# A graph layer on one core: who takes the mixed tiles out of PSUM and adds them to the rows

## What is computed

```python
xn = _layernorm(x, axis=-1)
x = x + _L0_gnn_ref(xn, edge_index, edge_weight, node_vec1) + _L0_mix_ref(xn[None], ...)[0]
x = x + _L0_ffn_ref(_layernorm(x, axis=-1)[None], ...)[0]
```

## Time and profile before

| what | us |
|---|---|
| median of 3 runs | 2407.29 (2406.35 to 2408.89) |
| the profiled execution: its time | 2410.31 |
| the profiled execution: its span | 2408.5 |
| front and setup, up to the first sort's hot_t | 0 to 247 |
| first sorts (with the mixed tiles from 267) | 247 to 382 |
| main loop and last units | 382 to 1905 |
| routing | 1905 to 1984 |
| experts | 1984 to 2408.5 |

### The profile page before, as it was taken

The page is one execution under the profiler, slowest core; times in us unless marked ns, Lnnn a source line. Parts: engine busy times, 40 slices in busy tenths (PEclk is TensorE's granted clock), DMA queues, the critical chain, the costliest instruction groups (busy, mean ns, idle before and its releaser), DMA issues. The chain is left out here.

```text
span 2408.5 us, 48312 instructions
## 1 busy us (share of the span) xinstructions
PE 2151.9 (89%) x16542; PEld 1889.3 (78%) x16543; DVE 2055.8 (85%) x3323; ACT 1214.5 (50%) x1686; POOL 1613.3 (67%) x1364
## 2 busy tenths in 40 slices
PE   3887579999999999999999999999999719999893
PEld 2555467888888888888888888888889619989893
DVE  5776889999999999999999999999888596666662
ACT  1222665555555555555555555555223146666661
POOL 1665005777777777777777777777777437888883
PEclk8998789999999999999999999999999869999997
DMA  6332333333322333333233333323355454444455
GB/s 168 83 84 61 97 105 108 90 91 95 93 89 89 93 90 89 91 98 91 89 94 88 89 90 99 92 89 87 106 153 148 138 147 81 76 77 77 75 76 135
DMA packets 167330, 235.54 MB, mean 98 GB/s; under 512 B 61084, under 2 KB 128007, under 8 KB 166948
## 3 DMA queue, kind: packets, MB, share of 16 engines
q0 software_dynamic: 70896, 164.43, 27.1%
q1 hardware_dynamic: 89584, 68.67, 9.7%
q10 hardware_dynamic: 6724, 0.83, 0.4%
HBM read 186.72 MB, written 53.51 MB: 100 GB/s over the span
## 5 line engine op out<-in xcount | busy, mean ns | idle before, releaser
L775 POOL DMA_INDIRECT picked<-xn_dram,place x1029 | 1160.7, 1128 | 506.5 <-issue 298.0
L851 PE MATMUL bank<-picked,pick_w 128*128 128x256 f32 x2058 | 500.4, 379 | 4.4 <-DMA picked<-xn_dram,place 4.4
L963 ACT COPY stage<-bank 128x512 f32<-128x512 f32 x343 | 200.5, 585 | 509.9 <-PE bank L839 495.4
L851 PEld LDWEIGHTS bank<-picked,pick_w 128*128 128x128 f32 x2058 | 390.9, 190 | 58.2 <-DVE pick_w L1154 5.1
L917 ACT COPY field_rep<-fields 128x1666 bf16 (+2 forms) x235 | 397.6, 1714 | 0.1
L847 PE MATMUL bank<-window,stage 128*128 128x256 f32 x1568 | 384.2, 388 | 0.0
L1147 DVE TENSOR_TENSOR hot_w<-hots,cur 128x1536 bf16<-128x1536 bf16 x343 | 328.6, 958 | 11.9
L847 PEld LDWEIGHTS bank<-window,stage 128*128 128x128 f32 x1568 | 284.8, 192 | 31.1
L1143 DVE TENSOR_TENSOR hots<-iota_j,cur 128x1408 bf16<-128x1408 bf16 x343 | 303.3, 884 | 0.0
L839 PE MATMUL bank<-hot_w,hots 128*128 128x128 bf16 x4116 | 287.2, 220 | 11.4 <-DVE hot_w L1147 7.6
L839 PEld LDWEIGHTS bank<-hot_w,hots 128*128 128x128 bf16 x4116 | 255.3, 99 | 47.4 <-DVE hot_w L1147 8.7
(11 more groups left out here) (245 smaller groups left out, 3396.6 us busy)
## 6 DMA issues: line engine op xcount, KB each, us to landing
picked<-xn_dram,place POOLq DMA_INDIRECT x1029
xn_dram<-xn SPq DMA_DIRECT2D x49, 128.0 KB, 1.7
xT_dram<-xT SPq DMA_DIRECT2D x49, 128.0 KB, 1.8
base_dram<-acc SPq DMA_DIRECT2D x7, 896.0 KB, 7.8
sum_dram<-acc SPq DMA_DIRECT2D x7, 896.0 KB, 4.4
z_dram<-vals SPq DMA_DIRECT2D x7, 896.0 KB, 8.5
out_dram<-sum_dram SPq DMA_DIRECT2D x1, 6250.0 KB, 22.0
w_all<-in_L_ffn_W_dram SPq DMA_DIRECT2D x8, 512.0 KB, 10.1
```

Of the source, the lines that this page charges most:

```text
L775: pool.indirect_dma_start(out=picked[:, i % SETS * PICK + q, :], out_offset=None, in_=xn_dram, in_offset=bass.IndirectOffsetOnAxis(ap=plac ...
L851: mm = pe.matmul(sum_ps[pp], pick_w[i % SETS][:, q, :], picked[:, i % SETS * PICK + q, :], start=False, stop=(q == PICK - 1))
L963: act.copy(block_sb[pp].rearrange("p j c -> p (j c)"), banks[pp][:, :]).then_inc(a_copied, 1)
```

## The change

Three things are changed in `edge_sum`. DVE's `add_mix` is removed at all its places. ACT gets `take_mix(t)`, which copies the bank to one of four buffers `mix_sb` in SBUF; these lie in hot_w2 and hot_w3, which the main loop first writes behind its wait for the stores. ACT's `sort` calls it three times ahead of the ranks, twice ahead of the tiles and twice ahead of the next fields. POOL adds the buffer to the row in acc, for all 49 tiles, ahead of the first gather, which now stands behind 49 adds rather than 42. PE waits for ACT's copy (`mix_taken`) where it waited for the add; ACT's copy of tile t waits for POOL's add of tile t - 4.

```diff
+        mix_sb = [hot_w[2 + i // 2][:, :, :, :].rearrange("p f j c -> p (f j c)").bitcast(F32)[:, i % 2 * D:(i % 2 + 1) * D] for i in range(4)]
...
         @block.gpsimd
         def _(pool):
-            pool.wait_ge(mix_added, (GRP - 1) * BU)
+            for t in range(NT):
+                pool.wait_ge(mix_taken, t + 1)
+                pool.tensor_tensor(acc[:, t, :], acc[:, t, :], mix_sb[t % 4], ALU.add).then_inc(mix_added, 1)
+            pool.wait_ge(mix_added, NT)
             for t in range(NG * NT):
...
                 if t >= 4:
-                    pe.wait_ge(mix_added, t - 3)
+                    pe.wait_ge(mix_taken, t - 3)
...
             def begin():
                 make_table(AHEAD - 1)
-                pe.wait_ge(mix_added, NT)
+                pe.wait_ge(mix_taken, NT)
                 blocks(0, 0, 0)
...
+            def take_mix(t):
+                act.wait_ge(mixed, t + 1)
+                if t >= 4:
+                    act.wait_ge(mix_added, t - 3)
+                act.copy(mix_sb[t % 4], mix_ps[t % 4]).then_inc(mix_taken, 1)
+
             def sort(s):
+                t = (s - 1) * BU
                 take_base(s)
...
+                for i in range(3 if s > 0 else 0):
+                    take_mix(t + i)
                 repeat_ranks(s)
+                for i in range(3, 5 if s > 0 else 3):
+                    take_mix(t + i)
                 repeat_tiles(s + 1)
+                for i in range(5, BU if s > 0 else 5):
+                    take_mix(t + i)
                 repeat_fields(s + 1, 0, 2)
...
-            def add_mix(t):
-                dve.wait_ge(mixed, t + 1)
-                dve.tensor_tensor(acc[:, t, :], acc[:, t, :], mix_ps[t % 4], ALU.add).then_inc(mix_added, 1)
-
             def sort(s):
-
-
-                t = (s - 1) * BU
                 in_row(s)
-                if s > 1:
-                    add_mix(t - 2)
-                    add_mix(t - 1)
                 rank_ahead(s)
                 rank(s)
                 values(s, 0, 2)
-                if later(s):
-                    add_mix(t)
-                    add_mix(t + 1)
                 values(s, 2, 4)
-                if later(s):
-                    add_mix(t + 2)
-                    add_mix(t + 3)
                 values(s, 4, FIELDS)
                 slots(s)
-                if later(s):
-                    add_mix(t + 4)
                 hot_tiles(s + 1)
...
             def begin():
-                add_mix(NT - 2)
-                add_mix(NT - 1)
                 dve.wait_ge(cur_done, 2)
```

More of the change, by code:

```diff
@@ L665, in turn_ps @@
             return banks[2 if n > LATE and n % 2 == 0 else 7][:, 0:D]
-        xT_in = [sem(f"xT_in{i}") for i in range(2)]; mixed = sem("mixed"); mix_added = sem("mix_added")
+        xT_in = [sem(f"xT_in{i}") for i in range(2)]; mixed = sem("mixed"); mix_taken = sem("mix_taken"); mix_added = sem("mix_added")
         small_in = sem("small_in"); z_out = [sem(f"z_out{i}") for i in range(2)]; stat_done = sem("stat_done")
```

## The result

The change makes the kernel slower: median 2418.39 us (2413.49 to 2421.28, 6 runs) against 2409.18 us for the kernel before in the same comparisons (2406.35 to 2411.80, 6 runs). The ratio is 1.0038, 95% interval 1.0025 to 1.0051, so +9.2 us. The profiled execution has a span of 2419.5 us, 11.0 more than the one before.

What follows compares the result with a forecast made beforehand. The sorts were taken as bound by a closed PE and DVE loop of 17.1 us. Six loops +7.0, last sort +1.0, late gathers +1.0 sum to +9.0: 2407.3 + 9.0 = 2416.3 us; own range 2409 to 2425, with rivals 2396 to 2424.

Steps and rivals of the forecast that it cites:

- The three terms of the sum: Six sort loops +7.0 us, the last sort +1.0, the later gathers on POOL +1.0.
- The first rival: In the sorts, DVE's bf16 operations do not meet POOL's adds; -10.2 us, so 2397 us; chance 0.22.
- the second: In the sorts, few adds meet DVE: three meetings cost 1.41 us, -0.24 a sort, 2407 us; chance 0.11.
- Six meetings: Between a table's landing and hot_t's end, six of seven POOL adds collide with DVE's two-SBUF-input operations; the seventh falls into slack.
- Their price, 0.47: In the sorts, what DVE pays in us per collision with a 256-column POOL add.
- The clock, taken as 0: PE's granted clock in base and table: change taken as 0, bounds -1.2 and +1.2 us a sort.
- The last sort: Table 8 waits for the slots: four adds removed, -1.32 us, five meetings, +2.35; net +1.0.
- What POOL is held from: Main loop's start: gathers stand behind all 49 adds, some 17 us later; +1.0 us, bounds 0 and +3.
- T: In each sort, the moment a table lands, from which the forecast counts times in us.
- The pace argument: In the main loop POOL needs 4.26 us a tile and PE 4.44, so POOL slowly regains its lead.
- ACT, taken as 0: In the sorts, ACT's seven copies, 2.6 us a sort, do not delay DVE: cost 0, bound +0.5 a sort.
- the ring of PE and DVE: Closed loop of each sort: 7.1 us on PE and 9.9 us on DVE, 17.1 us a sort.

Runs made afterwards that it cites:

- copies only: The changed kernel without POOL's adds: ACT still copies all 49 mixed tiles, POOL only counts them; 2390.05 us, ratio 0.9916.
- The better place for the adds: Kernel before with DVE's adds moved to the head of the next sort: 2397.10 us; changed kernel with POOL's adds held until hot_t: 2397.05 us.

## Why the prediction was right, and where it was not

**The answer and its cause held; that the sum came within 0.2 us is luck.** Forecast +9.0 us, measured +9.2. The three terms of the sum measured +10.1, +1.2 and +1.1, 12.4 where 9.0 stood, and the stages outside took some of it back: the profiled executions are 11.0 apart, the medians 9.2. The chain of the argument is borne out at each link: L511 in the front told what would happen to values, slots and hot_t; the runs with POOL idle and with POOL writing only show that the adds do it, and by reading. The first rival (bf16 operations do not meet POOL) is refuted by 1.56 us for hot_t, the second (few adds meet) by six meetings or seven in every sort. One sign came otherwise than written: a pair of values was to take 2.5 to 2.9 us. The pair in front of the first meeting keeps its 2.00, the pair behind it takes 3.06, with two meetings.

**Six meetings: right in six sorts, seven in sort 6. Their price, 0.47: too low by 0.06.** It was scaled from 0.44 for 238 columns; measured is 0.53 for 256 (11.41 - 8.23 = 3.18 in six). Net of the 1.65 that makes +1.53 a sort where +1.17 stood. This is the larger part, 2.2 us, of what the six loops show above the forecast, +10.1 and not +7.0; the seventh meeting of sort 6 is 0.5 more, and its late start of the values about 0.35.

**The clock, taken as 0: right for the sum of this change.** The tables took 4.54 to 5.93 us and not 5.08 to 5.64, and in all six loops 0.8 us less than before; the bases took 1.60 us each, 0.8 more. The granted clock over the sorts is 0.83 in both kernels. That the two cancel was not foreseen.

**The last sort: +1.0 forecast, +1.2 measured**, the price of the meeting again.

**What POOL is held from: this step failed.** It put +1.0 on the late gathers. +1.1 us do lie between the last table's start and the first picking matmul, but they are the table's: 6.30 us where the earlier trace rows have 5.17, behind a longer idle time of PE (4.12, not 2.65) and at a granted clock of 0.58, not 0.72. That the longer wait is what lowered the clock is argued; the run with early gathers shows only that the gathers did not do it. Timeline of the changed kernel:

```profile
389.42 6.30 PE L816 MATMUL bank<-vals,slot 128*128 128x245 bf16 x34 [4.12 <-issue]
391.68 1.21 POOL L779 DMA_INDIRECT picked<-xn_dram,place  x1 [0.30 <-POOL acc L768]
...
396.86 0.56 DVE L1153 TENSOR_TENSOR pick_w<-hots,cur_w 128x384 f32<-128x384 bf16 x1 [0.84 <-DMA base_dram<-acc]
...
399.04 0.94 PEld L855 LDWEIGHTS bank<-picked,pick_w 128*128 128x128 f32 x5 [0.31 <-DMA picked<-xn_dram,place]
```

The first gather came at T+12.3 (379.39 to 391.68), as forecast at T+12 (the picking matmul of before stood at T+17.3, not 17.4, as its T is 368.57; nothing hangs on it), and landed 0.3 us too late for PE's weights, and starting it 18 us earlier changed nothing. The pace argument held: POOL gained on PE from there, and the main loop is no longer than before.

**ACT, taken as 0: right for this change.** Neither the slots nor hot_t waited for ACT. It does copy `cur` 3.5 us later behind T of sort 7, but PE is still in its last table then. Where the sorts are shorter this is no longer hidden: DVE waits 4.2 us for it with copies only and with PE adding.

**The first rival's price was too mild.** I had the removal alone at 1.65 us a sort, with a remark that the clock could give more. It gives 3.4: with waits of 2.36 to 2.72 us PE stays at 2.4 GHz in five of six loops, and the loop's bound changes from the ring of PE and DVE to DVE alone. That would not have changed the forecast. The better place for the adds brought 10 to 11 us, with loops of 14.87 and 15.13 us; the kernel in which neither DVE nor POOL adds brought 21, with 13.61, of which 8 lie outside the sorts.

## What to carry to other kernels

An add that DVE makes from PSUM has one input in SBUF, and POOL's work passed such an operation by where the front has both (L533); the same add on POOL needs two, and costs a busy DVE 0.53 us for 256 f32 columns, more than the 0.33 it took on DVE. Before moving work to an idle engine, look for rows where that engine already runs beside the busy one, and compare the longest and the shortest duration of one and the same operation. If work must go, move it to a stretch where the bounding engine waits, or to an engine that reads elsewhere: an identity matmul took over the add of a tile for about 0.4 us of PE's time (1.30 us a tile, where two products alone took 0.9).

## What the runs showed of the hardware that was not expected

- POOL gets between two DVE operations also where they stand back to back with no wait between them: five values had three meetings in six sorts (6.46 - 4.85 = 3 x 0.54) and four in sort 6, the slots two and hot_t one. I had held it possible that it would not.
- A copy by POOL, which reads one input, costs DVE less than half of what an add costs, which reads two: 0.20 against 0.53 us for 256 f32 columns; an add of 128 columns costs 0.26.
- The clock can double what a saving gives. With POOL idle, PE waits 2.36 to 2.72 us ahead of the base and five of six tables take 3.81 us; before, with 3.85 us, they take 5.08 to 5.64. A saving of 1.65 us on DVE became 3.4 by this. The length of the wait does not decide it alone: the slow table among the six (4.68 us) stands behind a wait of 2.59 us and not behind the longest, and with POOL copying, PE waits 3.56 us, less than before, and the tables take 5.43 to 5.99.
